# A four-image attention kernel on one core: loads, stores and early statistics of its first block moved, and identity products put where TensorE waits around two changes of blocks

## What is computed

```python
x = x + _L0_conv_ref(_gn(x), ...)          # group norm; 8 heads, d = 16, rotation by sin and cos, mask, 5x5 depthwise conv of v
t = _to_tokens(x)
t = t + _L1_attn_ref(_ln_t(t), ...)        # one head of 128 channels over 2304 tokens of an image
t = t + _L1_ffn_ref(_ln_t(t), ...)         # 8 experts, two picked per image
```

## Time and profile before

| | us |
|---|---|
| median of 3 runs | 3588.86 (3587.58 to 3589.58) |
| profiled execution | 3589.26 |
| span of its profile, first to last instruction | 3587.5 |
| TensorE busy | 3430.1 (96%) |
| VectorE busy | 2622.8 (73%) |
| ScalarE busy | 2030.0 (57%) |
| GpSimd busy | 1647.8 (46%) |
| DMA moved | 308.47 MB, mean 86 GB/s |

### The profile page before, as it was taken

The page is one execution under the profiler, slowest core; times in us unless marked ns, Lnnn a source line. Parts: engine busy times, 40 slices in busy tenths (PEclk is TensorE's granted clock), DMA queues, the critical chain, the costliest instruction groups (busy, mean ns, idle before and its releaser), DMA issues. The chain is left out here.

```text
span 3587.5 us, 96344 instructions
## 1 busy us (share of the span) xinstructions
PE 3430.1 (96%) x30684; PEld 2653.5 (74%) x30684; DVE 2622.8 (73%) x6494; ACT 2030.0 (57%) x3660; POOL 1647.8 (46%) x862
## 2 busy tenths in 40 slices
PE   6599999999999999999999999999699999999988
PEld 4377777777777777777777777777477777878867
DVE  6588888888888888888888888888565564644457
ACT  3366666666666666666666666666345454454533
POOL 4565666556565556565566555665300101005112
PEclk9899999999999999999999999999799999999989
DMA  6732232233224224222423422322520110000011
GB/s 198 248 102 96 92 107 96 93 100 102 94 92 132 71 95 133 77 84 99 129 68 100 127 92 69 101 92 67 156 69 29 42 57 12 31 1 1 1 41 43
DMA packets 111227, 308.47 MB, mean 86 GB/s; under 512 B 11512, under 2 KB 72875, under 8 KB 90315
## 3 DMA queue, kind: packets, MB, share of 16 engines
q1 hardware_dynamic: 110507, 306.48, 27.6%
q10 hardware_dynamic: 584, 0.26, 0.0%
HBM read 252.38 MB, written 54.31 MB: 85 GB/s over the span
## 5 line engine op out<-in xcount | busy, mean ns | idle before, releaser
L757 DVE CUSTOM_DVE_ANT_0 c_S<-c_Sps,mask_tiles 128x768 f32<-128x768 f32 x1728 | 1619.3, 956 | 425.8 <-PE c_Sps L808 366.9
L698 ACT ACTIVATE c_PT<-c_Tps 128x512 f32<-128x512 f32 x2592 | 1428.8, 604 | 871.6 <-PE c_Tps L819 809.0
L669 POOL TENSOR_SCALAR c_S<-c_S,c_row_max 128x2304 f32<-128x2304 f32 x576 | 1413.8, 2454 | 946.3 <-DVE c_row_max L768 946.3
L819 PE MATMUL c_Tps<-ident,c_S 128*128 128x128 f32 x10368 | 1399.3, 273 | 4.1 <-ACT c_PT L698 4.1
L819 PEld LDWEIGHTS c_Tps<-ident,c_S 128*128 128x128 f32 x10368 | 1225.9, 140 | 151.5 <-ACT c_PT L698 9.7
L808 PE MATMUL c_Sps<-c_K,c_Q 96*128 (+1 forms) x3456 | 853.5, 328 | 44.4 <-DVEq L738 27.3
L832 PE MATMUL c_Ops<-c_PT,c_V 128*32 128x256 f32 x10368 | 619.1, 382 | 0.8 <-ACT c_PT L698 0.8
L832 PEld LDWEIGHTS c_Ops<-c_PT,c_V 128*32 128x32 f32 x10368 | 307.4, 109 | 243.7 <-issue 50.4
L808 PEld LDWEIGHTS c_Sps<-c_K,c_Q 96*128 96x128 bf16 x3456 | 314.8, 98 | 203.5 <-issue 144.4
L1359 DVE TENSOR_SCALAR_CACHE_REDUCE l_S<-l_Sps 128x384 f32<-128x384 f32 x432 | 240.4, 557 | 293.9 <-PE l_Sps L1182 267.2
L1095 ACT ACTIVATE ln2T<-l_Tps 128x384 f32<-128x384 f32 x432 | 196.6, 491 | 404.6 <-PE l_Tps L1203 404.6
(11 more groups left out here) (204 smaller groups left out, 1662.2 us busy)
## 6 DMA issues: line engine op xcount, KB each, us to landing
mask_tiles<-in_mask SPq DMA_DIRECT2D x144, 1152.0 KB, 7.7
numerators<-c_O SPq DMA_DIRECT2D x288, 64.0 KB
mask_tiles<-numerators SPq DMA_DIRECT2D x7, 2304.0 KB, 8.6
q_parts<-f_parts SPq DMA_DIRECT2D x12, 576.0 KB, 7.6
k_parts<-f_parts SPq DMA_DIRECT2D x12, 576.0 KB
c_Q<-q_parts SPq DMA_DIRECT2D x71, 96.0 KB
c_vpad<-v_padded SPq DMA_DIRECT2D x8, 756.0 KB, 15.0
c_K<-k_parts SPq DMA_DIRECT2D x7, 864.0 KB, 8.7
```

The lines of the kernel that those rows point to most:

```text
L669: pool.tensor_scalar(S[:, slot, :], S[:, slot, :], -1.0, row_max[:, slot:slot + 1], ALU.mult, ALU.add).then_inc(shifted, 1)
L698: act.activation(dst, src, ACT.Exp, scale=-1.0).then_inc(exp_done, 1)
L757: dve.tensor_tensor_reduce(out=S[:, r % ROW_SLOTS, cols(CH, c)].rearrange("p (k n) -> p k n", k=2), in0=Sps[:, n % S_SLOTS, :, 0:GW], in1= ...
L819: last = pe.transpose(Tps[:, g % T_SLOTS, cols(P, k)], S[:, (2 * b + t) % ROW_SLOTS, cols(P, kt)], ident[:, :])
```

## The change

The change touches three blocks.

- Front: the angles come ready for 128 partitions from HBM, in three column pieces on separate semaphores, instead of two loads that repeat 16 rows eight times. The small weights are loaded from ScalarE's queue. x has three slots. The mask is loaded early, for two of the four mask tiles. The early loads of the second block stand behind the stores, for images 0 and 1 alone. Statistics start a unit earlier in two groups a unit, and `normalise` stands one unit earlier. For the last image all of v is made in its first three units and stored at once.
- Core: heads of images 2 and 3 and two mask tiles are loaded at its start. The denominators of image 0 are loaded at its end.
- Attention: the sums of both halves stand ahead of the wait for the small matmuls.
- `keep_busy` issues float32 products of the identity with itself, 128 columns each: 52 behind the last unit of the front block in four portions, 2 behind each of the nine lead chunks, 20 at the end of the core block, 28 and 4 ahead of the spreading, 28 behind the first projection.

```diff
+def keep_busy(pe, bank, ident, count):
+
+    for _ in range(count):
+        pe.matmul(bank[:, 0:P], ident[:, :], ident[:, :], start=True, stop=True)
...
-        XT = sb("XT", [P, 2, N])
+        X_SLOTS = 3
+        XT = sb("XT", [P, X_SLOTS, N])
...
+        def v_work(b, step):
+
+            if b == B - 1:
+                return [(image, 2 * step + g) for image in (False, True) for g in range(2)] if step < NCH else []
+            return [(step >= NCH, 2 * (step % NCH) + g) for g in range(2)]
...
-            sp.dma_start(cosT[:, :], s["cosT"].unsqueeze(0).to_broadcast([HEADS, D, N])).then_inc(angles_in, 16)
-            sp.dma_start(sinT[:, :], s["sinT"].unsqueeze(0).to_broadcast([HEADS, D, N])).then_inc(angles_in, 16)
+            for c in range(NCH):
+                sp.dma_start(cosT[:, cols(CH, c)], s["cosT"][:, cols(CH, c)]).then_inc(angles_in[c], 16)
+                sp.dma_start(sinT[:, cols(CH, c)], s["sinT"][:, cols(CH, c)]).then_inc(angles_in[c], 16)
             load_x(1)
+            for it in range(2):
+                sp.dma_start(mask[:, it, :], s["mask"][it]).then_inc(mask_in, 16)
+            load_x(2)
             for b in range(B):
                 if b:
                     store_parts(b - 1, 1)
                 store_v(b)
-                if b:
+                if b == B - 1:
+                    store_vpad(b)
+                store_parts(b, 0)
+                if b < B - 1:
+                    store_vpad(b)
+                if b + X_SLOTS < B:
+                    sp.wait_ge(mm_ready, 2 * STEPS * (b + 1))
+                    load_x(b + X_SLOTS)
+                if b in (1, 2):
                     load_early(b - 1)
-                sp.dma_start(mask[:, b, :], s["mask"][b]).then_inc(mask_in, 16)
-                store_parts(b, 0)
-                store_vpad(b)
-                if b + 2 < B:
-                    sp.wait_ge(mm_ready, 2 * STEPS * (b + 1))
-                    load_x(b + 2)
...
+            pe.wait_ge(vps_taken, VPS_USES * B)
+            keep_busy(pe, vps[:, 0, :], ident, 16)
+            pe.wait_ge(sum_ready, LAST + 1)
+            keep_busy(pe, vps[:, 0, :], ident, 10)
+            pe.wait_ge(d1_last, 1)
+            keep_busy(pe, vps[:, 0, :], ident, 8)
+            pe.wait_ge(p3_last, 1)
+            keep_busy(pe, vps[:, 0, :], ident, 18)
...
-                    if b + 1 < B and step == STEPS - 1:
+                    if b + 1 < B and step == 4:
                         normalise(b + 1)
                     with_sin(u)
-                    if b + 1 < B and step in (1, 2):
-                        statistics(b + 1, range(NG // 2 * (step - 1), NG // 2 * step))
+                    if b + 1 < B and step < 3:
+                        statistics(b + 1, range(2 * step, 2 * step + 2))
...
-            sp.sem_inc(mask_in, 32 * 2)
+            sp.sem_inc(mask_in, 32)
+            sp.sem_inc(k_in, 48)
+            sp.sem_inc(q_in, 48)
+            sp.sem_inc(v_in, 16)
+            load_first_head(sp, s, K, Q, V_next, 2, [image_in[2]] * 3)
             load_half(0)
-            load_first_head(sp, s, K, Q, V_next, B - 1, (k_in, q_in, v_in))
-            sp.wait_ge(q_in, 48)
+            load_first_head(sp, s, K, Q, V_next, 3, [image_in[3]] * 3)
+            load_mask(1)
             load_q(1)
...
             for r in range(LEAD):
                 for c in range(NCH):
                     scores(0, 0, r, c, first=True)
+                    keep_busy(pe, Tps[:, 0, :], ident, 2)
...
+            keep_busy(pe, Tps[:, 2, :], ident, 10)
+            pe.wait_ge(den_in, 16)
+            keep_busy(pe, Tps[:, 2, :], ident, 10)
+            pe.wait_ge(inv_ready, 1)
+            keep_busy(pe, Tps[:, 2, :], ident, 8)
             pe.wait_ge(weights_in, 16 * 8)
...
             sum_first_pairs(0)
             invert(0)
+            sum_first_pairs(1)
             sum_first(0)
+            sum_first(1)
             dve.wait_ge(small_ready, 1)
```

More of the change, by code:

```diff
@@ L132, in layer0_front @@
         small = vps[:, 0, :]
-        weights_in, angles_in, mask_in = sem("weights_in"), sem("angles_in"), sem("mask_in")
-        x_first, x_in = sem("x_first"), [sem("x0_in"), sem("x1_in")]
+        weights_in, mask_in = sem("weights_in"), sem("mask_in")
+        angles_in = [sem(f"angles{c}_in") for c in range(NCH)]
+        x_first, x_in = sem("x_first"), [sem(f"x{b}_in") for b in range(B)]
         constants, prep, scaled_k, rotated_w = sem("constants"), sem("prep"), sem("scaled_k"), sem("rotated_w")
@@ L312, in second_part @@
                 act.activation(parts[:, m, 1, cols(CH, c)], rot_sum[:, m, cols(CH, c)], ACT.Copy).then_inc(p2_ready, 1)
+            for i, w in enumerate((a["Wq"], None, a["Wk"], None, a["Wv"])):
+                if w is not None:
+                    act.dma_start(weights[:, i, :], w).then_inc(weights_in, 16)
+            for i, v in enumerate((a["bq"], None, a["bk"], None, a["bv"], a["dw_b"])):
+                if v is not None:
+                    act.dma_start(rows[:, i, :], v.rearrange("(a n) -> a n", a=1)).then_inc(weights_in, 16)
+            act.dma_start(taps_row[:, :], a["dw_w"].rearrange("a b o c -> (a b o) c")).then_inc(weights_in, 16)
             act.wait_ge(constants, 2)
@@ L320, in _ @@
                     u = STEPS * b + step
-                    for g in range(2):
-                        if step < NCH:
-                            take_v(b, 2 * step + g)
-                        else:
-                            take_v_image(b, 2 * (step - NCH) + g)
-                        if g == 0 and u:
+                    for k, (image, g) in enumerate(v_work(b, step)):
+                        if k == 1 and u:
                             first_part(u - 1)
+                        (take_v_image if image else take_v)(b, g)
+                    if not v_work(b, step):
+                        first_part(u - 1)
                     if u > 1:
                         second_part(u - 2)
-                    if step == STEPS - 2 and b + 1 < B:
+                    if step == 3 and b + 1 < B:
                         deviation(b + 1)
@@ L373, in project @@
                 for k in range(2):
-                    last = pe.matmul(mm[:, use % MM_SLOTS, k, 0:GW], weights[:, 2 * m + r, :], XT[:, b % 2, cols(GW, 2 * c + k)],
+                    last = pe.matmul(mm[:, use % MM_SLOTS, k, 0:GW], weights[:, 2 * m + r, :], XT[:, b % X_SLOTS, cols(GW, 2 * c + k)],
                                      start=True, stop=True)
@@ L392, in _ @@
                         pe.wait_ge(norm_step, 3)
-                    for g in range(2):
-                        if step < NCH:
-                            v_tokens(b, 2 * step + g)
-                        else:
-                            v_image(b, 2 * (step - NCH) + g)
+                    for image, g in v_work(b, step):
+                        (v_image if image else v_tokens)(b, g)
                     if step == 3 and b + 1 < B:
                         group_means(b + 1)
+            pe.wait_ge(vps_taken, VPS_USES * B)
[6 more added lines that the diff above has]
+            keep_busy(pe, vps[:, 0, :], ident, 18)
         @block.vector
@@ L678, in place_v @@
                 images = cols(B // 2 * TILES, half)
-                if not first or half:
+                if not first:
                     act.wait_ge(v_in, 16 * (h + 1))
+                elif half:
+                    act.wait_ge(image_in[2], 16 * EARLY_LOADS)
+                    act.wait_ge(image_in[3], 16 * EARLY_LOADS)
                 act.activation(V[:, images, 0:D], V_next[:, images, :], ACT.Copy).then_inc(v_placed, 1)
@@ L799, in scores @@
             def scores(ip, p, r, c, first=False):
-                if c == 0 and r == (ROWS - 2 if first else 0):
+                if r == 0 and c == 0 and not first:
                     pe.wait_ge(q_in, 48 * (ip + 1))
                     pe.wait_ge(k_in, 48 * (ip // HEAD_PAIRS + 1))
+                if first and c == 0 and r in (4, 6):
+                    pe.wait_ge(image_in[r // 2], 16 * EARLY_LOADS)
                 n = NCH * r + c
@@ L1868 @@
     "xT": lambda x: x.reshape(B, N, C).transpose(0, 2, 1),
-    "sinT": lambda x: x.reshape(N, D).T,
-    "cosT": lambda x: x.reshape(N, D).T,
+    "sinT": lambda x: np.tile(x.reshape(N, D).T, (HEADS, 1)),
+    "cosT": lambda x: np.tile(x.reshape(N, D).T, (HEADS, 1)),
 }
```

83 lines of the change are left out of this document (43 added, 40 removed).

## The result

| | before | changed |
|---|---|---|
| median of 5 runs each, us | 3588.86 | 3568.99 |
| lowest to highest, us | 3584.49 to 3589.58 | 3568.51 to 3572.09 |
| ratio of the two, 95% interval | | 0.9948 [0.9935, 0.9962] |
| the profiled execution, and its span, us | 3589.26, 3587.5 | 3568.51, 3566.7 |

The account below looks back on a forecast made before the run. TensorE bounds the unchanged loop; front-block waits, stores in the gap and the second block change could move. Savings 14.3 + 12 + 11 + 0 + 2.3 = 39.6 us from 3589.26 gave 3550, with an 8-in-10 range of 3539 to 3561.

Parts of the forecast that it names:

- Term A: Start of the front block: earlier angle pieces let the fourth unit start at 27.5 instead of 41.80, 14.3 us saved.
- Term B: Front block from fourth unit to last unit's end: fewer waits for x, `normalise` and clock, 12 us saved, bounds 5 and 15.
- a part of 0.59 MB takes 2.9 us on half the engines: Front block: price of one k part's store, taken from a rate of 205 GB/s at a DMA share of 0.50.
- The count of 22 to 23.4 us an image: Front block: time the DMA half used by k is busy per image, against 23.5 us for the units.
- Term C: Gap from the front block's last unit to the next block's first matmul: 16.5 instead of 27.3 us, 11 saved.
- the stores bind fully: Rival, front block and gap: front units save 5, gap 8, start 13; 28.3 us in all, 3561; chance 0.15.
- Term D: Lead chunks and first pair: padded image's wait against transposes at full clock, 0 us, from -2 to +4.
- Term E: Second change of blocks, into attention: quicker GpSimd adds and full-clock transposes save 2.3 us, from 0 to 4.
- The slower loop: Rival, loop over pairs: moved buffers could slow each pair; at 0.75 us a pair, 14 us slower, 3604; chance 0.02.

Follow-up runs that it names:

- the control: The changed kernel run again with no edit: 3568.62 us, ratio 0.9942 to the kernel before.
- experiment 4: The changed kernel with the second half's sums put back behind the attention block's small products: 3568.71 us, ratio 0.9946.
- experiment 6: The kernel before with only 128-row angle tables, loaded in three pieces before the second x, and weights issued by ScalarE: 3579.95 us, ratio 0.9975.
- Experiment 2: The changed kernel with k scratch laid out so each k store has 128 equal outermost rows, and six k loads: 3554.09 us, ratio 0.9909.
- experiment 3: The changed kernel with image 3's v work spread over six units and its padded image stored last: 3563.91 us, ratio 0.9936.
- experiment 1: The changed kernel without any products of the identity: 3567.58 us, ratio 0.9945.
- experiment 9: The changed kernel with the attention block's two loads of x issued ahead of all others: 3568.57 us, ratio 0.9943.

## Why the prediction was wrong

**Term A was right**: 14.2 of 14.3 at the fourth unit, and 12 to 13.4 in the later profiles with the same start (28.37 in the control, 29.68 in experiment 4). What it left out is that this gain lasts only where something else lets it (experiment 6).

**Term B failed in the step "a part of 0.59 MB takes 2.9 us on half the engines".** The rate of 205 GB/s was read from the window of 162 to 164, in which more than one k part was travelling; the same trace has 104 GB/s from 158 to 160, with all three issued. One alone takes 6.3 to 6.7 us from issue to landing at a share of 0.37, where the sum had 4.5. The count of 22 to 23.4 us an image on that half stood just under the 23.5 of the units; 2 us more on each of three k parts make it 28 to 29, an estimate. The waits were 1.90, 4.82 and 2.19 us, and the second of them came with a fall of the clock. Experiment 2, in which the k stores are no longer held to half a share, has none of the three. The working held the warning itself: two numbers within a few per cent of each other, of which one was an estimate. A second step was missing: image 3's v work was moved ahead, and nothing in the sum asked when the padded image's buffer would be free (3.93 us at 102.61, 5.62 in the control). In the units this weighed about as much as the first: from the start of the last image to its last unit's end it is 30.5 us (91.87 to 122.35), and 26.4 in experiment 3 (92.12 to 118.53).

**Term C failed by the same price.** Its 15 us behind the last unit took 8.7 for three k parts and 1.6 to land. SP's timeline and its waits in the changed kernel, which answer to the earlier trace rows:

```profile
127.42 6.22 SPq L219 DMA_DIRECT2D k_parts<-f_parts  x3
```

```profile
SPq L254 <- DMA k_parts<-f_parts: 9.6, 1, 9.6
```

That is 15.8 us from the first issue to the last landing, with the rest of a q part in it, for the 10.3 of the sum. Three parts at the price of the lone one, 3 x 4.7 + 1.6 us to land, come to 15.7. With wide stores the last unit ends at 117.7 and the lead starts at 131.1; the forecast had 116.3 and 133. So the order of events was right, and the store's price was the error. The rival "the stores bind fully" had the mechanism; its B of 5 came (6.1), its C of 8 did not (4.9).

**Term D** was forecast at 0 between -2 and +4 and was -2.4. The wait for the padded image behind seven loads was foreseen as 1 us and was 1.5; behind it the last chunk waited 2.83 us. The clock was at half at the lead's start, as feared, and the first chunks with their two identity products came every 1.5 us, where the lead had 1.20 a chunk before; without these products the lead was 1.1 us shorter (experiment 1). The Trainium skill was quoted on this part ("TensorE: Matmul & The Clock Gate", section "What's actually happening"): it puts the penalty of the ramp under 1% of a typical kernel's span and advises against fitting to a specific count of cold products; of products issued only to hold the clock that section says nothing. That D stays at 0 does not follow from it, since 1% of this kernel is 36 us, more than any term of the sum. The runs agree on the size: with the identity products there was at best no difference (experiment 1), at worst they were 3.8 to 6.9 of 3550 us slower, 0.1 to 0.2%.

**Term E** had the wrong sign, -2.0 for 2.3. It counted that the spreading would run at full clock. It ran at half (8.04 us for its twelve records), as in the kernel before (twice 4.20 for six): TensorE had stood idle for 2.9 us until `spread` was ready, and the clock was down again when the spreading began. The faster GpSimd that the term counted on did not come either: its six adds took 8.04 us for 8.02 before, with VectorE's products with the spread inverses at the same time in both; in experiment 9, where VectorE waited, they took 5.73. The loss itself is 0.8 us up to VectorE's first add, since x landed later behind the first sum, and 1.2 behind it, where the second part of the projection ran at half clock (4.58 us for its 24 records, 3.26 before and in experiment 1).

**The slower loop** was refuted: 2367.20 us in both.

## What to carry to other kernels

Price a transfer by one that travels alone, with the shape it has in DRAM: two stores of the same bytes took 3.5 and 6.5 us, and the layout of one scratch tensor was worth 12 to 15 us, where the whole change was worth 20. When a sum says that a resource is busy for nearly as long as the work above it, treat it as the bound and fix it first. Products issued to keep TensorE's clock up in a wait bought nothing here: at the two changes of blocks the clock was down again when the real work began or after its next idle 2.5 to 3 us, and once the stores were faster the products themselves held up the block's end.

## What was unexpected of the hardware

A k part's store, 8 blocks as its outermost dimension, alone kept the engines at a share of 0.37 and moved 107 GB/s; three queued moved up to 210 at 0.51; with 128 rows as the outermost dimension a window had 389. The Trainium skill ("DMA: Bandwidth & Descriptors", section "Rules for kernel authors") confines such a store to at most 8 of the 16 engines; the share of 0.51 in the queue agrees. Alone it is 0.37, half of the 0.74 that a lone q part had.

GpSimd's eight small products took 4.73 and 6.08 us beside a quieter VectorE, and 7.33 to 9.51 beside its sums, in two profiles of the same kernel.

TensorE was busy 13.87 of 16.70 us at half clock from 2543.3 to 2560.0, directly behind a stretch at full clock with 2.9 us idle in it, while the kernel without the identity products was at 0.56 and then 0.72 over the same work.
